# A four-layer attention chain with a state-space scan on one core: the scan as two chains of 64 batches, and another order of DMAs at the beginning and the end

## The chip, the cores and the metric

The kernel runs on one core of one Trainium2 chip. The metric is the device time of the whole program in microseconds; the kernel before has a median of 4145.38 us over 3 runs (4143.74 to 4145.70). A core has five engines that run side by side and wait for each other by semaphores: TensorE (PE in the profile, its weight loads PEld), VectorE (DVE), ScalarE (ACT), GpSimd (POOL) and SyncE (SP), which here issues nearly all DMAs. A DMA can also be issued by ACT.

## The reference

128 batches with sequences of 128 tokens of 256 features; all in float32. Four layers follow one another, each attending to the same context or to the state before:

```python
x = L0(x, ctx)         # causal self-attention, 16 heads; cross-attention; feed-forward; three layer norms
x = L1(ctx, x, ...)    # norm, attention to itself, gelu(fc1) of 4 channels, fc2, norm, attention again
x = L2(x, ctx)         # H_real + softmax(H_real @ H_fake.T) @ H_fake
# L3: multi-head attention on normed inputs, a residual, and then
xn = _layernorm(x, g2, beta2)
U = (xn @ W_in.T + b_in) @ Bmat                      # 64 states per token
def step(s, u_t):
    s = jax.nn.silu(s @ A.T) + u_t
    return (s, s)
_, states = jax.lax.scan(step, zeros, U.transpose(1, 0, 2))   # over the 128 tokens
ssm_out = jnp.einsum('tbs,sh->bth', states, Cmat)
mod = program_probs.mean(axis=1) @ W_prog.T + b_prog          # program_probs: 128 x 128 x 64
return x + ssm_out + mod[:, None, :]
```

The scan is sequential over tokens and independent over batches.

## The kernel before, in words

The batches are worked in 64 groups of G = 2. `drive` runs every engine through 64 + 6 iterations, each with one step of every unit (`self_in`, `self_att`, `ctx_in`, `ctx_att`, `ffn`, `pair`, `real`, `mix_in`, `mix_att`, `mix_out`) for a group that lags by a fixed number of iterations; the order inside an iteration comes from the table PROGRAM, and eight PSUM banks are lent by the table BANKS. `drive` also calls extra functions ahead of a given iteration (its last argument).

Beginning. SP loads what the first attention needs (`first_loads`), then at iteration 1 the context weights (`load_ctx_weights`, L450) and at iteration 2 everything else (`load_late_weights`, L454): nine weights, 29 small rows and columns, and 16 pieces of the columns q3_b and k3_b (L462). All of these count on the semaphore `rest_in`. At iteration 3 (`PREPARED`) each engine runs `prepare()`: ACT reorders the weights q2, k2, q3, k3 (L1018) once all of `rest_in` has come; TensorE and DVE fold norms into weights and biases and make the modulation rows. For these program_probs is summed over its 128 tokens: four pieces of 1 MB (`probs_in`), loaded from ACT's queue at iteration 2 (L1026), one pair added by DVE (L1338), the other by POOL (L1543, semaphore `half_added`), their sum by DVE (L1341) and so on. The rows of all batches are stored to memory at iteration 6 and come back group by group (`load_mod`, L497, tile `mod`).

End of the loop. For each group SP loads the modulation rows, stores the finished residual (`store`, L502, tensor `residual`) and the two batches' u of 64 states by 128 tokens (`store_u`, L518, tensor `u_turned`). At iteration 68 `scan_early` (L504) waits until the buffers that the scan takes over are free and loads u (L443, tile `shared`, in the code `fresh`) and the first two residual chunks (L445, tile `turned`, in the code `res_t`) of the first 122 batches; after the last group the other 6 batches follow, and chunks 2 and 3 (L527). A chunk is 8 tokens of all 128 batches, 1 MB.

Scan. A second block. The state has 64 rows, below it 64 rows of u_t, so that one matmul of 128 rows with A.T twice over gives (silu + u) A.T: recurrence matmul L1612, Silu L1632 into the next column block of `gu` (tiles Z and X), and the output matmul L1604 with C, which DVE adds into the residual chunk (L1641). POOL copies u for four tokens at a time into `gu` (L1625). SP stores finished chunks and loads those to come (L1583, L1579). A float32 matmul is two passes, shown as two records.

Of the kernel before, what the change touches and what calls it, by code (L numbers as in the profile page):

```python
# [24 lines left out]
G = 2  # L25
# [220 lines left out]
PREP_BANKS = (0, 1, 2, 3, 4, 5)  # L246
# [16 lines left out]
def build(nc, dram):  # L263
# [6 lines left out]
    with ExitStack() as ctx:  # L270
# [99 lines left out]
        means, added, half_added, ordered = (sem(n) for n in ("means", "added", "half_added", "ordered"))  # L370
# [34 lines left out]
        def row(t):  # L405
# [7 lines left out]
        late_loads = [*((wt[n][:], weight(n)) for n in ("fc1", "fc2")), *((in_rows[n], weight(n)) for n in ("q3", "k3")),  # L413
                      *((wt[n][:], weight(n)) for n in ("v3", "o3")), (w_gate[:], weight("gate")), (w_in[:], weight("in")),
                      (b_mat[:, :, 0:NS], dram["b_mat"].rearrange("(a p) n -> p a n", p=128)),
                      *((t[:], dram["col_" + n]) for n, t in cols.items() if n not in ("q3_b", "k3_b")),
                      *((t[:], row(dram["row_" + n])) for n, t in rows.items() if n[0:3] not in ("ln1", "ln2")),
                      *((gate_col[32 * b:32 * b + 4, :], dram["gate_b"].rearrange("(c o) -> c o", o=1)) for b in range(G)),
                      *((w_cross[32 * b:32 * b + 5, :], dram["w_cross"]) for b in range(G)),
                      (w_prog[0:NP, 0, :], dram["w_prog"]), (w_prog[:, 1, :], row(dram["prog_b"])),  # L420
                      *((a_two[NS * k:NS * k + NS, 0:NS], dram["a_t"]) for k in range(2)),
                      *((c_two[NS * k:NS * k + NS, :], dram["c_mat"]) for k in range(2))]
        FIRST = 16 * len(first_loads)
        REST = 16 * (len(ctx_loads) + len(late_loads) + 8 * DH)
# [10 lines left out]
        vbank, obank = pbank[0:2], pbank[2:6]  # L435

        u_in, zeroed, u_ready, v_ready, g_ready, o_ready, out_ready = (
            sem(n) for n in ("u_in", "zeroed", "u_ready", "v_ready", "g_ready", "o_ready", "out_ready"))
# [1273 lines left out]
```

## Time and profile before

| what | value |
|---|---|
| median of 3 runs | 4145.38 us (4143.74 to 4145.70) |
| the profiled execution | 4143.41 us, of which the span of the trace is 4141.6 us |
| PE busy | 3924.8 us, 95% |
| ACT busy | 3527.3 us, 85% |
| DVE busy | 3346.5 us, 81% |
| POOL busy | 2858.1 us, 69% |
| DMA | 159.99 MB, 39 GB/s in the mean |
| granted TensorE clock, mean | 0.98 |

The busy figures are sums over engines that overlap; a busy TensorE is not one at its peak, since the ends of its matmuls are modelled. The span begins with the first instruction on the core and ends with the last; the device time is 1.8 us longer. The loop over the groups takes most of it, and a share over the whole span says little on the beginning, the last groups and the scan, so these were read from stretches of the trace.

### The profile page before, as it was taken

What the parts mean: (1) busy time and instruction counts of PE and PEld (TensorE: products, weight loads), DVE (VectorE), ACT (ScalarE), POOL (GpSimd) and SP (SyncE); (2) the same over time, 40 slices, a digit from 0 to 9 for tenths busy, and PEclk for the clock granted to TensorE, in tenths of its full rate; (3) what the DMA queues carried; (4) which work ended last, traced back from release to release, by engine and by line L of the source; (5) the groups of instructions that cost most, each with busy time, mean ns of one, the idle gap of its engine ahead of it and who ended that gap; (6) DMA issues with size and microseconds to landing.
All of it is one profiled execution on the core that took longest, in us unless ns stands there. A gap on an engine that the chain in (4) does not pass through costs nothing.

```text
span 4141.6 us, 110586 instructions
## 1 busy us (share of the span) xinstructions
PE 3924.8 (95%) x36667; PEld 3225.8 (78%) x36667; DVE 3346.5 (81%) x9518; ACT 3527.3 (85%) x8333; POOL 2858.1 (69%) x3173
## 2 busy tenths in 40 slices
PE   5899999999999999999999999999999999999759
PEld 4678888888888888888888888888888888887635
DVE  4688888888888888888888888888888888888534
ACT  3799999899999999999999999999999998999522
POOL 2567777777777777777777777777777777776634
PEclk7999999999999999999999999999999999999869
DMA  3010011011101101110101011001100110110037
GB/s 114 19 32 25 28 31 33 20 33 31 34 20 31 33 26 28 31 34 20 34 31 33 20 31 33 27 27 31 34 25 29 31 33 20 34 31 26 15 104 274
DMA packets 121843, 159.99 MB, mean 39 GB/s; under 512 B 12282, under 2 KB 108356, under 8 KB 116612
## 3 DMA queue, kind: packets, MB, share of 16 engines
q1 hardware_dynamic: 120708, 148.74, 11.9%
q8 instruction: 303, 4.96, 0.5%
q10 hardware_dynamic: 576, 4.19, 0.2%
q14 instruction: 256, 2.10, 0.2%
HBM read 115.01 MB, written 37.88 MB: 37 GB/s over the span
## 4 chain that ended last, share of the span: by engine, by line
PE 71%; ACT 17%; issue 6%; DVE 1%; POOL 1%; DMA 0%; ACTq 0%; SPq 0%; DVEq 0%; another core or an unknown queue 0%; POOLq 0%
PE bank L544 18%; PE bank L600 11%; PE bank L552 8%; PE bank L536 7%; PE bank L571 5%; PE bank L717 4%; ACT probT L920 3%; PE bank L763 3%; PE bank L704 3%; PE bank L634 3%; PE bank L647 3%; ACT L901 2%; PE bank L629 2%; ACT prob L901 2%; ACT HC L970 1%
## 5 line engine op out<-in xcount | busy, mean ns | idle before, releaser
L600 PE MATMUL bank<-ident,prob 128*128 128x128 f32 x5120 | 728.6, 277 | 67.3 <-ACT CR L987 26.8
L920 ACT ACTIVATE probT<-bank 128x512 f32<-128x512 f32 x1280 | 730.5, 593 | 70.1 <-PE bank L600 68.7
L600 PEld LDWEIGHTS bank<-ident,prob 128*128 128x128 f32 x5120 | 590.9, 142 | 148.8 <-issue 62.6
L891 ACT ACTIVATE turned<-bank 128x512 f32<-128x512 f32 x896 | 538.9, 602 | 186.8 <-PE bank L536 177.5
L1120 DVE TENSOR_REDUCE mx<-bank 128x4 f32<-128x512 f32 x768 | 507.6, 682 | 187.0 <-PE bank L571 184.6
L909 ACT ACTIVATE prob<-prob,mx 128x128 f32<-128x128 f32 x2048 | 650.6, 396 | 3.9 <-DVE mx L1109 3.8
L544 PE MATMUL bank<-turned,shared 128*128 128x256 f32 x2560 | 617.0, 384 | 1.2 <-ACT turned L891 1.1
L1426 POOL TENSOR_TENSOR rs_ln<-ve_ln,half 128x2 f32<-128x2 f32 x320 | 227.3, 710 | 444.5 <-DVE ve_ln L1091 444.5
L1131 DVE TENSOR_TENSOR prob<-bank,mx 128x512 f32<-128x512 f32 x768 | 520.5, 685 | 15.3 <-PE bank L600 1.9
L544 PEld LDWEIGHTS bank<-turned,shared 128*128 128x128 f32 x2560 | 470.2, 192 | 69.2 <-issue 12.1
L901 ACT ACTIVATE prob<-prob 128x512 f32<-128x512 f32 x768 | 475.6, 636 | 13.6 <-DVE prob L1131 12.7
L571 PE MATMUL bank<-shared,turned 32*128 32x256 f32 x4096 | 447.6, 402 | 3.6 <-DVE prob L1102 2.2
L1505 POOL TENSOR_SCALAR shared<-turned,half_of 128x512 f32<-128x512 f32 x256 | 399.8, 1575 | 21.4 <-ACT turned L891 21.3
L1102 DVE TENSOR_TENSOR prob<-bank,causal 128x512 f32<-128x512 f32 x512 | 344.6, 683 | 54.9 <-PE bank L600 47.7
L552 PE MATMUL bank<-shared,turned 128*128 128x256 f32 x1536 | 369.9, 384 | 1.2 <-DVE turned L1238 1.2
L1109 DVE TENSOR_REDUCE mx<-prob 128x4 f32<-128x512 f32 x512 | 346.9, 678 | 16.8
L571 PEld LDWEIGHTS bank<-shared,turned 32*128 32x128 f32 x4096 | 284.1, 185 | 82.4 <-issue 47.4
L552 PEld LDWEIGHTS bank<-shared,turned 128*128 128x128 f32 x1536 | 281.5, 190 | 55.7 <-issue 22.7
L634 PE MATMUL bank<-probT,shared 128*32 128x128 f32 x8192 | 290.9, 277 | 0.9 <-ACT probT L920 0.8
L1440 POOL TENSOR_TENSOR X<-X,row_ln_g 128x512 f32<-128x512 f32 x192 | 244.8, 1275 | 62.0 <-ACT X L970 62.0
L1516 POOL TENSOR_TENSOR prob<-prob,inv 128x512 f32<-128x512 f32 x256 | 263.3, 1039 | 4.3 <-DVE inv L1147 4.3
L634 PEld LDWEIGHTS bank<-probT,shared 128*32 128x32 f32 x8192 | 204.5, 109 | 76.4 <-issue 75.3
(238 smaller groups left out, 9003.1 us busy)
## 6 DMA issues: line engine op xcount, KB each, us to landing
shared<-in_x SPq DMA_DIRECT2D x128, 256.0 KB, 3.0
CB<-in_ctx SPq DMA_DIRECT2D x64, 256.0 KB, 4.0
CC<-in_ctx SPq DMA_DIRECT2D x64, 256.0 KB, 2.7
mod<-mod_rows SPq DMA_DIRECT2D x64, 256.0 KB, 3.7
residual<-X SPq DMA_DIRECT2D x64, 256.0 KB, 3.2
out<-turned SPq DMA_DIRECT2D x16, 1024.0 KB, 4.8
turned<-residual SPq DMA_DIRECT2D x14, 1024.0 KB, 6.8
u_turned<-us SPq DMA_DIRECT2D x128, 32.0 KB, 2.2
```

The costliest lines, as they stand in the source:

```text
L544: last = nc.tensor.matmul(t[:, m * W:(m + 1) * W], w[:, a, m * 128:(m + 1) * 128], src[:, a, :], start=(a == 0), stop=(a == DH - 1))
L552: last = nc.tensor.matmul(t[:, b * D:(b + 1) * D], src[:, a, b * S:(b + 1) * S], w[:, a, :], start=(a == 0), stop=(a == DH - 1))
L571: last = nc.tensor.matmul(t[:, a * W:(a + 1) * W], QT[p][rows_, a, b * S:(b + 1) * S], KEYS[p][rows_, a, :, b * S:(b + 1) * S], start=True ...
L600: last = nc.tensor.transpose(t[:, h * 128:(h + 1) * 128], src[:, h, :], ident[:])
L634: last = nc.tensor.matmul(t[k * 32:(k + 1) * 32, r * 128:(r + 1) * 128], VP[p][:, b, 4 * r + k, :], src[:, k, :], start=True, stop=True)
L891: nc.scalar.activation(dst, banks.of(f"{unit}.{name}")[:, 0:n], ACT.Copy).then_inc(*st["act"].mark(name))
L901: nc.scalar.activation(flat(t), flat(t), ACT.Exp, scale=SCALE[p]).then_inc(*st["act"].mark(f"exp.{b}{r}"))
L909: last = nc.scalar.activation(t[:, h, :], t[:, h, :], ACT.Exp, bias=low[:, h:h + 1], scale=1.0)
L920: nc.scalar.activation(flat(t), banks.of(f"{att}.turn.{b}{r}")[:, :], ACT.Copy).then_inc(*st["act"].mark(f"probT.{b}{r}"))
L1120: nc.vector.tensor_reduce(m[:], banks.of(f"{att}.tile.{b}{r}")[:, :].rearrange("p (h t) -> p h t", h=4), AX, ALU.max)\
L1131: nc.vector.tensor_tensor(t[:], banks.of(f"{att}.tile.{b}{r}")[:, :].rearrange("p (h t) -> p h t", h=4), maxes.of(f"{att}.max.{b}{r}")[:]. ...
L1505: last = nc.gpsimd.tensor_scalar(KEYS[p][:, :, c, :], KT[p][:], half_of[:, c:c + 1], None, ALU.mult)
```

## The change

Three parts, in one diff.

Beginning: the 7 context loads and 9 late weights are issued from ACT's queue before ACT's first instruction of the loop, and the 4 loads of program_probs right after its first reordering. SP issues the 29 small loads at iteration 1 and the 16 pieces at iteration 2. The second pair of program_probs is added by DVE. The products of `prepare()` stand in three banks in place of six.

End: `scan_early` is called by `load_mod` behind the modulation rows of group 62. `scan_late` loads what is missing of groups 61 and 62 ahead of the last store. The u of groups 62 and 63 is copied from its tile straight into the scan's buffer, and the last group's rows of chunk 0 straight from the residual tile `X6`.

Scan: each step is done for two halves h of 64 batches, with PSUM banks and semaphores of their own. The output of half 1 goes to the upper 64 partitions of the same bank.

```diff
@@ -243,7 +243,7 @@
-PREP_BANKS = (0, 1, 2, 3, 4, 5)
+PREP_BANKS = (0, 1, 2)
...
@@ -447,14 +449,12 @@
-                def load_ctx_weights():
-                    for t, src in ctx_loads:
+                def load_small():
+                    sp.wait_ge(prep, 2)
+                    for t, src in small_loads:
                         sp.dma_start(t, src).then_inc(rest_in, 16)
-                def load_late_weights():
-                    sp.wait_ge(prep, 2)
-                    for t, src in late_loads:
-                        sp.dma_start(t, src).then_inc(rest_in, 16)
+                def load_biases():
...
+                    if g == NG - 2:
+                        scan_early()
                 def store(g):
+                    if g == NG - 1:
+                        scan_late()
                     for w in latest(mix_out["pool"].done("mod", g)):
                         sp.wait_ge(*w)
                     sp.dma_start(res_g[g], nat["X6"][:]).then_inc(res_out.sem, 16)
+                    if g == NG - 1:
+                        for b in range(G):
+                            sp.dma_start(res_t[0][B - G + b:B - G + b + 1, :, :], nat["X6"][0:TC, b, :]).then_inc(res_in[0], 16)
...
+                def scan_late():
+                    for w in latest(u_out.done(NG - 3), res_out.done(NG - 2)):
+                        sp.wait_ge(*w)
+                    sp.dma_start(fresh[:, EARLY:EARLY + G, :], u_t[:, EARLY:EARLY + G, :]).then_inc(u_in, 16)
+                    for k in (0, 1):
+                        sp.dma_start(res_t[k][EARLY:B - G, :, :], res_d[EARLY:B - G, k * TC:(k + 1) * TC, :]).then_inc(res_in[k], 16)
                 def store_u(g):
                     for w in latest(mix_out["dve"].done("u", g)):
                         sp.wait_ge(*w)
                     for b in range(G):
-                        sp.dma_start(u_g[g][b], us[NS * b:NS * b + NS, :]).then_inc(u_out.sem, 16)
+                        to = u_g[g][b] if g < NG - 2 else fresh[:, G * g + b, :]
+                        sp.dma_start(to, us[NS * b:NS * b + NS, :]).then_inc(u_out.sem, 16)
...
                                    pair=dict(load=load_pair), mix_out=dict(load=load_mod, store=store, store_u=store_u)), "sp",
-                      {1: load_ctx_weights, 2: load_late_weights, MOD_STORED: store_modulation, NG + LAGS - 2: scan_early})
-                for w in latest(res_out.done(NG - 1), u_out.done(NG - 1)):
+                      {1: load_small, 2: load_biases, MOD_STORED: store_modulation})
+                for w in latest(res_out.done(NG - 1)):
                     sp.wait_ge(*w)
-                scan_input(sp, slice(EARLY, B), (0, 1))
+                sp.dma_start(res_t[1][B - G:B, :, :], res_d[B - G:B, TC:2 * TC, :]).then_inc(res_in[1], 16)
                 for k in (2, 3):
                     sp.dma_start(res_t[k], res_d[:, k * TC:(k + 1) * TC, :]).then_inc(res_in[k], 16)
...
                                                         scale=L0_HD ** -0.5 if name == "q1" else 1.0)
                         last.then_inc(ordered, 1)
-                def load_probs():
-                    ctxb_v = ctxb_d.rearrange("b (c s) n -> b c s n", c=4)
-                    for c, t in enumerate(probs_in):
-                        act.dma_start(t, ctxb_v[:, c, :, :]).then_inc(probs_here, 16)
                 def prepare():
                     act.wait_ge(rest_in, REST)
                     in_order("q2", "k2", "q3", "k3")
+                for t, src in ctx_loads + late_weights:
+                    act.dma_start(t, src).then_inc(rest_in, 16)
                 act.wait_ge(first_in, FIRST)
                 in_order("q1", "k1")
+                ctxb_v = ctxb_d.rearrange("b (c s) n -> b c s n", c=4)
+                for c, t in enumerate(probs_in):
+                    act.dma_start(t, ctxb_v[:, c, :, :]).then_inc(probs_here, 16)
...
                     dve.wait_ge(probs_here, 64)
                     t = probs_in[0]
                     nc.vector.tensor_tensor(t, t, probs_in[1], ALU.add).then_inc(added, 1)
-                    dve.wait_ge(added, 1)
-                    dve.wait_ge(half_added, 1)
+                    nc.vector.tensor_tensor(probs_in[2], probs_in[2], probs_in[3], ALU.add).then_inc(added, 1)
+                    dve.wait_ge(added, 2)
                     nc.vector.tensor_tensor(t, t, probs_in[2], ALU.add).then_inc(added, 1)
                     for k in range(4):
                         n = S // 8 >> k
-                        dve.wait_ge(added, k + 2)
+                        dve.wait_ge(added, k + 3)
                         nc.vector.tensor_tensor(t[:, 0:n, :], t[:, 0:n, :], t[:, n:2 * n, :], ALU.add).then_inc(added, 1)
-                    dve.wait_ge(added, 6)
+                    dve.wait_ge(added, 7)
                     nc.vector.tensor_tensor(msum[:, 1, 0:NP], t[:, 0, :], t[:, 1, :], ALU.add).then_inc(means, 2)
...
                 def rows_here():
-                    pool.wait_ge(probs_here, 64)
-                    nc.gpsimd.tensor_tensor(probs_in[2], probs_in[2], probs_in[3], ALU.add).then_inc(half_added, 1)
                     pool.wait_ge(rest_in, REST)
...
-                def output(n):
-                    if n >= 4:
+                def output(n, h):
+                    if n >= 4 and h == 0:
                         pe.wait_ge(out_ready, n - 3)
-                    nc.tensor.matmul(obank[n % 4][:, 0:D], gu[n // 4 % 4][:, n % 4, :], c_two[:], start=True, stop=True).then_inc(o_ready, 1)
+                    nc.tensor.matmul(obank[n % 4][side[h], 0:D], gu[n // 4 % 4][:, n % 4, side[h]], c_two[:], start=True, stop=True)\
+                        .then_inc(o_ready, 1)
                 pe.wait_ge(zeroed, 1)
                 for n in range(1, S):
                     if (n - 1) % 4 == 0:
                         pe.wait_ge(u_ready, (n - 1) // 4 + 1)
-                    if n >= 2:
-                        pe.wait_ge(g_ready, n - 1)
-                    nc.tensor.matmul(vbank[n % 2][:, 0:B], a_two[:], gu[(n - 1) // 4 % 4][:, (n - 1) % 4, :], start=True, stop=True)\
-                        .then_inc(v_ready, 1)
-                    output(n - 1)
-                pe.wait_ge(g_ready, S - 1)
-                output(S - 1)
+                    for h in range(2):
+                        if n >= 2:
+                            pe.wait_ge(g_ready[h], n - 1)
+                        nc.tensor.matmul(vbank[h][n % 2][0:NS, 0:B // 2], a_two[:, 0:NS], gu[(n - 1) // 4 % 4][:, (n - 1) % 4, side[h]],
+                                         start=True, stop=True).then_inc(v_ready[h], 1)
+                        output(n - 1, h)
+                for h in range(2):
+                    pe.wait_ge(g_ready[h], S - 1)
+                    output(S - 1, h)
             @block.gpsimd
             def _(pool):
                 pool.wait_ge(u_in, 32)
+                for w in latest(u_out.done(NG - 1)):
+                    pool.wait_ge(*w)
                 for c in range(S // 4):
                     if c >= 4:
-                        pool.wait_ge(o_ready, 4 * (c - 4) + 4)
+                        pool.wait_ge(o_ready, 8 * (c - 4) + 8)
                     nc.gpsimd.tensor_scalar(gu[c % 4][NS:2 * NS, :, :], fresh[:, :, 4 * c:4 * c + 4].rearrange("p b t -> p t b"),
                                             1.0, None, ALU.mult).then_inc(u_ready, 1)
             @block.scalar
             def _(act):
                 for n in range(1, S):
-                    act.wait_ge(v_ready, n)
-                    nc.scalar.activation(gu[n // 4 % 4][0:NS, n % 4, :], vbank[n % 2][0:NS, 0:B], ACT.Silu).then_inc(g_ready, 1)
+                    for h in range(2):
+                        act.wait_ge(v_ready[h], n)
+                        nc.scalar.activation(gu[n // 4 % 4][0:NS, n % 4, side[h]], vbank[h][n % 2][0:NS, 0:B // 2], ACT.Silu).then_inc(g_ready[h], 1)
             @block.vector
                 def add(n, k, kb, t):
-                    dve.wait_ge(o_ready, n + 1)
+                    dve.wait_ge(o_ready, 2 * n + 2)
                     nc.vector.tensor_tensor(res_t[kb][:, t, :], res_t[kb][:, t, :], obank[k][:, 0:D], ALU.add).then_inc(out_ready, 1)
                 def body(c, k, r):
                     for t in range(TC):
                         n = c * TC + t
                         if t == 1:
-                            dve.wait_ge(res_in[k], 16 * (r + (2 if k < 2 else 1)))
+                            dve.wait_ge(res_in[k], 16 * (r + (4, 3, 1, 1)[k]))
                         if at_least(n, 1):
```

On TensorE, the scan's first steps. Z is the tile of states and u, a_two is A.T, c_two is C. Before:

```order
L1612 MATMUL bank<-Z,a_two 128x128 [waits u_ready,zeroed]
L1604 MATMUL bank<-c_two,Z 128x256
L1612 MATMUL bank<-Z,a_two 128x128 [waits g_ready]
L1604 MATMUL bank<-c_two,Z 128x256
L1612 MATMUL bank<-Z,a_two 128x128 [waits g_ready]
L1604 MATMUL bank<-c_two,Z 128x256
```

And of the changed kernel, where L1631 is the recurrence and L1621 the output:

```order
L1631 MATMUL bank<-Z,a_two 64x64 [waits u_ready,zeroed]
L1621 MATMUL bank<-c_two,Z 64x256
L1631 MATMUL bank<-Z,a_two 64x64
L1621 MATMUL bank<-c_two,Z 64x256
L1631 MATMUL bank<-Z,a_two 64x64 [waits g_ready0]
L1621 MATMUL bank<-c_two,Z 64x256
L1631 MATMUL bank<-Z,a_two 64x64 [waits g_ready1]
L1621 MATMUL bank<-c_two,Z 64x256
```

The recurrence of each half waits for the Silu of its own half only, and stands behind the output of the other half.

On SP's queue, the last groups of the loop before (L497 modulation rows, L502 residual out, L518 u out, L443 and L445 the scan's u and residual in, L527 chunks 2 and 3):

```order
L443 DMA shared<-u_turned 64x15616 [waits ctx_in_dve_3,self_att_pe_2,ctx_att_pe_4,self_att_pool_2,ffn_pe_4,self_in_dve_2,u_out,self_in_pool_1,res_out,self_in_dve_1,self_in_pe_1]
L445 DMA turned<-residual 122x2048 x2
L497 DMA mod<-mod_rows 128x512 [waits mix_out_pool_6]
L502 DMA residual<-X 128x2x256 [waits mix_out_pool_6]
L518 DMA u_turned<-us 64x128 [waits mix_out_dve_6]
L518 DMA u_turned<-us 64x128
L497 DMA mod<-mod_rows 128x512 [waits mix_out_pool_6]
L502 DMA residual<-X 128x2x256 [waits mix_out_pool_6]
L518 DMA u_turned<-us 64x128 [waits mix_out_dve_6]
L518 DMA u_turned<-us 64x128
L443 DMA shared<-u_turned 64x768 [waits u_out,res_out]
L445 DMA turned<-residual 6x2048 x2
```

The same place in the changed kernel (L506 residual out, L536 u out, L445, L447 and L526, L528 the scan's inputs, L510 the direct copies):

```order
L497 DMA mod<-mod_rows 128x512 [waits mix_out_pool_6]
L445 DMA shared<-u_turned 64x15616 [waits ctx_in_dve_3,self_att_pe_2,ctx_att_pe_4,self_att_pool_2,ffn_pe_4,self_in_dve_2,u_out,self_in_pool_1,res_out,self_in_dve_1,self_in_pe_1]
L447 DMA turned<-residual 122x2048 x2
L506 DMA residual<-X 128x2x256 [waits mix_out_pool_6]
L536 DMA shared<-us 64x128 [waits mix_out_dve_6]
L536 DMA shared<-us 64x128
L497 DMA mod<-mod_rows 128x512 [waits mix_out_pool_6]
L526 DMA shared<-u_turned 64x256 [waits res_out,u_out]
L528 DMA turned<-residual 4x2048 x2
L506 DMA residual<-X 128x2x256 [waits mix_out_pool_6]
L510 DMA turned<-X 1x8x256 x2
L536 DMA shared<-us 64x128 [waits mix_out_dve_6]
```

Group 62's modulation rows stand ahead of the two loads of 122 rows, those of group 63 still behind them, and u goes to `shared` instead of `u_turned`.

On ACT, the beginning of the changed kernel (before, the table load and the first reordering were its first instructions, and the loads of in_ctxb came behind four evacuations):

```order
L1046 DMA w_v<-in_w_v 128x2x256
L1046 DMA w_o<-in_w_o 128x2x256
L1046 DMA w_gate<-in_w_gate 128x2x4
L1046 DMA X<-in_w_in 128x2x256
L1046 DMA H<-in_b_mat 128x2x64
L1036 ACT_TABLE_LOAD
L1036 ACTIVATE shared<-turned 128x256 [waits first_in]
L1036 ACTIVATE shared<-turned 128x256 x3
L1051 DMA shared<-in_ctxb 128x2048 x3
L1051 DMA turned<-in_ctxb 128x2048
```

These are the last five of its 16 weight loads; ACT's first activation stands behind all of them.

## Rows read from the trace of the kernel before

**Rows 1.** The page: shares of the last chain; groups, as busy, mean ns.

```profile
PE 71%; ACT 17%; issue 6%; DVE 1%; POOL 1%; DMA 0%; ACTq 0%; SPq 0%; DVEq 0%; another core or an unknown queue 0%; POOLq 0%
...
L920 ACT ACTIVATE probT<-bank 128x512 f32<-128x512 f32 x1280 | 730.5, 593 | 70.1 <-PE bank L600 68.7
...
L634 PE MATMUL bank<-probT,shared 128*32 128x128 f32 x8192 | 290.9, 277 | 0.9 <-ACT probT L920 0.8
```

**Rows 2.** Stretches: length, then busy PE, PEld, DVE, ACT, POOL, clock, DMA, GB/s.

```profile
40.20:60.20 20.00, 0.07 (x4) 0.00 (x0) 0.00 (x0) 3.10 (x10) 0.00 (x0) 0.58 0.37 77
...
87.70:3930.00 3842.30, 3727.01 (x35603) 3092.28 (x35604) 3230.78 (x9230) 3438.52 (x8083) 2755.14 (x3102) 0.99 0.10 28
...
4030.10:4137.30 107.20, 106.18 (x494) 64.15 (x493) 52.58 (x125) 33.27 (x123) 54.59 (x29) 1.00 0.72 265
```

**Rows 3.** Timeline, beginning: start, length, instruction, [idle before it and releaser].

```profile
4.61 0.47 SPq L452 DMA_DIRECT2D turned<-in_w_q  x1
...
6.71 1.34 ACT L1018 ACTIVATE shared<-turned 128x256 f32<-128x256 f32 x4 [4.70 <-DMA NF<-in_causal]
...
18.29 0.38 SPq L476 DMA_DIRECT2D shared<-in_x  x1
...
21.66 3.76 SPq L457 DMA_DIRECT2D w_v<-in_w_v  x1
...
52.28 3.67 SPq L462 DMA_DIRECT2D col_k_b<-in_col_k_b  x8
57.15 1.34 ACT L1018 ACTIVATE shared<-turned 128x256 f32<-128x256 f32 x4 [16.89 <-DMA col_k_b<-in_col_k_b]
...
60.24 1.11 PE L647 MATMUL bank<-ident,outT 128*128 128x128 f32 x4 [19.98 <-ACT outT L935]
```

**Rows 4.** Timeline, the preparation on DVE.

```profile
65.53 2.28 DVE L1338 TENSOR_TENSOR shared<-shared 128x2048 f32<-128x2048 f32 x1
...
72.43 3.27 DVE L1341 TENSOR_TENSOR shared<-shared 128x2048 f32<-128x2048 f32 x1 [4.62 <-POOL shared L1543]
```

**Rows 5.** Timeline, the last groups of the loop.

```profile
3937.07 33.36 SPq L497 DMA_DIRECT2D mod<-mod_rows  x1
...
3989.07 0.18 DVE L1147 RECIPROCAL inv<-den 128x4 f32<-128x4 f32 x1
3995.80 1.26 POOL L1539 TENSOR_TENSOR X<-X,mod 128x512 f32<-128x512 f32 x1 [24.40 <-issue]
...
3998.23 4.03 POOL L1516 TENSOR_TENSOR prob<-prob,inv 128x512 f32<-128x512 f32 x4
...
4012.23 1.26 POOL L1539 TENSOR_TENSOR X<-X,mod 128x512 f32<-128x512 f32 x1 [1.35 <-ACT H L970]
```

**Rows 6.** DMA from 3957 to 3994: queue's packets, MB, share; issue, KB, landing.

```profile
q1 hardware_dynamic: 366, 2.18, 14.4%
...
mod<-mod_rows SPq DMA_DIRECT2D x1, 256.0 KB, 58.6
```

**Rows 7.** The chain that ended last, before the scan: start, length, what.

```profile
4016.24 1.90 DMA u_turned<-us
...
4018.21 4.17 DMA shared<-u_turned
```

**Rows 8.** Timeline, one step of the scan.

```profile
4080.48 0.27 ACT L1632 ACTIVATE X<-bank 64x128 f32<-64x128 f32 x1 [0.58 <-PE bank L1612]
4080.80 0.30 PEld L1612 LDWEIGHTS bank<-X,a_two 128*128 128x128 f32 x2 [0.33 <-ACT X L1632]
...
4081.33 0.27 ACT L1632 ACTIVATE Z<-bank 64x128 f32<-64x128 f32 x1 [0.58 <-PE bank L1612]
```

**Rows 9.** Lines L1612 and L1604: duration ns min/median/max, first and last start, shape.

```profile
L1612 PE MATMUL bank<-Z,a_two x128: 275/348/552, 4024.5 to 4129.4; 128*128 128x128 f32 x128
...
L1604 PE MATMUL bank<-c_two,Z x128: 379/382/634, 4025.1 to 4129.8; 128*128 128x256 f32 x128
```

**Rows 10.** DMA from 4060 to 4120: queue's packets, MB, share of 16 engines.

```profile
q1 hardware_dynamic: 2497, 18.23, 83.5%
```

More of the change, by code:

```diff
@@ L369, in build @@
         first_in, rest_in, probs_here, prep, mods, turned_b = (sem(n) for n in ("first_in", "rest_in", "probs_here", "prep", "mods", "turned_b"))
-        means, added, half_added, ordered = (sem(n) for n in ("means", "added", "half_added", "ordered"))
+        means, added, ordered = (sem(n) for n in ("means", "added", "ordered"))
         steps = {u: {e: Steps(sem, u, e) for e in ENGINES} for u in UNITS}
@@ L412, in build @@
                      *((rows[n][:], row(dram["row_" + n])) for n in ("ln1_g", "ln1_b", "ln2_g", "ln2_b"))]
[L413 to L422, printed above, removed]
+        late_weights = [*((wt[n][:], weight(n)) for n in ("fc1", "fc2")), *((in_rows[n], weight(n)) for n in ("q3", "k3")),
+                        *((wt[n][:], weight(n)) for n in ("v3", "o3")), (w_gate[:], weight("gate")), (w_in[:], weight("in")),
+                        (b_mat[:, :, 0:NS], dram["b_mat"].rearrange("(a p) n -> p a n", p=128))]
@@ new lines, in build @@
+        small_loads = [*((t[:], dram["col_" + n]) for n, t in cols.items() if n not in ("q3_b", "k3_b")),
+                       *((t[:], row(dram["row_" + n])) for n, t in rows.items() if n[0:3] not in ("ln1", "ln2")),
+                       *((gate_col[32 * b:32 * b + 4, :], dram["gate_b"].rearrange("(c o) -> c o", o=1)) for b in range(G)),
+                       *((w_cross[32 * b:32 * b + 5, :], dram["w_cross"]) for b in range(G)),
+                       (w_prog[0:NP, 0, :], dram["w_prog"]), (w_prog[:, 1, :], row(dram["prog_b"])),
+                       *((a_two[NS * k:NS * k + NS, 0:NS], dram["a_t"]) for k in range(2)),
+                       *((c_two[NS * k:NS * k + NS, :], dram["c_mat"]) for k in range(2))]
@@ L434, in build @@
                  for n in range(NB)]
-        vbank, obank = pbank[0:2], pbank[2:6]
-        u_in, zeroed, u_ready, v_ready, g_ready, o_ready, out_ready = (
-            sem(n) for n in ("u_in", "zeroed", "u_ready", "v_ready", "g_ready", "o_ready", "out_ready"))
+        vbank, obank = (pbank[0:2], pbank[6:8]), pbank[2:6]
+        u_in, zeroed, u_ready, o_ready, out_ready = (sem(n) for n in ("u_in", "zeroed", "u_ready", "o_ready", "out_ready"))
+        v_ready, g_ready = ([sem(f"{n}{h}") for h in range(2)] for n in ("v_ready", "g_ready"))
+        side = [slice(B // 2 * h, B // 2 * h + B // 2) for h in range(2)]
         res_in = [sem(f"res_in{n}") for n in range(NB)]
@@ L790, in prepare @@
                 def prepare():
-                    b_cols, b_v3, b_u, b_ub, b_turn, b_o = (pbank[n] for n in PREP_BANKS)
+                    b_fold, b_mod, b_o = (pbank[n] for n in PREP_BANKS)
                     for w in latest(*(banks.free(n) for n in PREP_BANKS)):
@@ L823, in prepare @@
                     for a in range(DH):
-                        last = nc.tensor.transpose(b_turn[:, a * 128:(a + 1) * 128], rows["v3_b"][:, a * 128:(a + 1) * 128], ident[:])
+                        last = nc.tensor.transpose(b_fold[:, a * 128:(a + 1) * 128], rows["v3_b"][:, a * 128:(a + 1) * 128], ident[:])
                     last.then_inc(turned_b, 1)
                     pe.wait_ge(means, 4)
-                    nc.tensor.matmul(b_u[:, 0:D], msT[0:NP, 0, 0:128], w_prog[0:NP, 0, :], start=True, stop=True).then_inc(means, 1)
+                    nc.tensor.matmul(b_mod[:, 0:D], msT[0:NP, 0, 0:128], w_prog[0:NP, 0, :], start=True, stop=True).then_inc(means, 1)
                     pe.wait_ge(turned_b, 2)
@@ L1332, in prepare @@
                 def prepare():
-                    b_cols, b_v3, b_u, b_ub, b_turn, b_o = (pbank[n] for n in PREP_BANKS)
+                    b_fold, b_mod, b_o = (pbank[n] for n in PREP_BANKS)
                     dve.wait_ge(rest_in, REST)
```

34 lines of the change are left out of this document (17 added, 17 removed).

## The prediction

> **What bounds the kernel now.** I read the page first: TensorE holds 71% of the chain that ended last [rows 1]. Most of that is the loop over 64 groups, which the change leaves as it is: 3842.3 us between 87.7 and 3930 [rows 2]. What can move is the 299.3 us around it, so I took a table of stretches next and looked for low TensorE shares: 0.07 us of work from 40.20 to 60.20, and the scan, 107.2 us with TensorE counted busy all through [rows 2]. The timeline, narrowed to beginning, end of the loop and scan, gave the rest.
>
> In the beginning TensorE stands 19.98 us behind an evacuation of ScalarE (ACT); ACT waits 16.89 us for the last bias column, col_k_b [rows 3]. SP issues these loads one by one until 55.95 us, some 0.47 us each, and 3.76 for one that found the queue full [rows 3]. It is bound by issue, not by bytes.
>
> At the end of the loop SP's load of group 62's modulation rows takes 33.36 us to issue and 58.6 to land [rows 5, 6]. It is queued behind two residual loads of 122 rows, during which the queue's packets fill 14.4% of the 16 engines [rows 6]: about two of them. POOL waits 24.40 us for it [rows 5].
>
> The scan step is a ring: Silu 0.27, 0.05 to the weight load, and from there 0.53 to the next Silu (4080.80 to 4081.33) [rows 8]. That is 0.85. Over the whole stretch it is 0.86: 494 passes, four a step, fill 106.18 us [rows 2]; the rest is the wait for a new block of u every fourth step.
>
> **Beginning.** Sixteen weight loads go from SP to ACT's queue and are issued from 0.7 us on. SP issues its 29 small loads where it had the context weights (4.61 us [rows 3]): 29 by 0.47 is 13.6, so the next group's x leaves at about 18.3, as it did (18.29). The 16 bias columns take 16 by 0.46 (3.67 for eight [rows 3]), from 19.2 to 26.6. With landing and a fuller queue all is there at about 31 instead of 57. ACT came to its wait at 57.15 - 16.89 = 40.26. Without the wait TensorE resumes at 40.26 + (60.24 - 57.15) = 43.4 [rows 3]. But ACT has 16 DMAs to issue before its first activation, 16 by 0.47 = 7.5 us: that moves from 6.71 to 9 at the earliest, and to 15 if two issues stall as SP's did. The four probability loads (1.9 us) now stand ahead of its first evacuation. I take +5 (3 to 8): TensorE resumes at 48.4, -11.9. In the preparation DVE waits 4.62 us for POOL's half of a sum [rows 4]; it does that add itself now, in 2.28 like its own of that size: -2.3. Both stand on the chain to the loop. Beginning: -14 (8 to 19). That the preparation uses three banks in place of six costs nothing: it has the same products in the same order, each in a part of a bank of its own.
>
> **End of the loop.** The modulation load of group 62 goes ahead of the residual loads and lands at once. Then DVE is late next: its last reciprocal ends at 3989.07 + 0.18 = 3989.25. Three of POOL's four scalings (4.03 / 4 = 1.01 each) are done by then, the last ends at 3990.3 instead of 3998.23 + 4.03 = 4002.26: -12 [rows 5]. Group 63's rows now queue behind the slow loads, which end by 3937.07 + 58.6 = 3995.7; they are needed at 4012.23 - 12 = 4000.2, so 4.5 us of cover remain [rows 5, 6]. The last u went to memory (1.90) and came back (4.17) [rows 7]; one DMA now puts it into the scan's buffer, at 1.9 to 2.5: -4, and +0.5, since SP issues three DMAs more ahead of it. End: -15.5 (12 to 17).
>
> [...]
>
> **Scan.** A step has four matmuls instead of two: for each half the recurrence, 64x64, and the output with 64 weight columns; and two Silus of 64 columns. A pass of 256 columns has 382 ns, the shortest of 128 has 275 [rows 9]: 0.84 ns a column and 168 ns from the last column to the end. Passes of 64 columns stream in 0.053. The ring of one half is Silu 0.216 (0.27 for 128 columns and 0.593 for 512 [rows 1, 8], so 0.84 ns a column), 0.05, and 0.53 less three times 0.053, 0.37: 0.64. Every matmul is two passes. The array's first 64 columns hold both recurrences and the output of half 0: 4 by 0.053 and 2 by 0.214, 0.64, with an uncovered weight load 0.67. The output of half 1 uses the other 64 columns and can run beside them, if tiles overlap. They do: 8192 passes of 128 columns on tiles of 32 cost 290.9 us [rows 1], 0.036 each where one alone streams 0.106. What no row shows is when a waiting engine is told, if a later instruction on another tile ends first.
>
> DMA has a floor of its own: 83.5% of 60 us in the scan [rows 10], 69.8 steps: 0.72 us a step if the engines never rest, 0.80 with a tenth of idleness. The ends are 0.67 and 0.92 (rival A). I take 0.77, between the two DMA figures: (0.86 - 0.77) by 127 = -11.4. What runs beside it still fits: an add of DVE and half a us of POOL's copies a step. Behind the last step the stores are less far along than now: +1. Scan: -10.4 (-23 to +9).
>
> **Sum** against the profiled execution of 4143.41 (span 4141.6): 4143.4 - 14 - 15.5 - 10.4 = 4103.5. The median of the runs shown, 4145.4, is 2 us above that execution, which makes 4105.
>
> **Rivals.**
> A. Passes end in program order, across tiles too. The next recurrence of half 0 can't end before the output of half 1 ahead of it: 0.107, 0.427, and the second output with half of it uncovered, 0.85 with a weight load and up to 0.92 a step. The scan is 8 slower, not 11 faster: 4105 + 19 = 4124. With no overlap at all it is 4 by 0.053 and 4 by 0.214, 1.09 with loads: +29, 4146. For A: in before no tile's product is waited for while another tile works. Against it: the 0.036 us. 0.15 for the two.
> [...]
> B. DMA decides the scan. Stores and loads hold each other up and a chunk comes late: 0.80 to 0.86 a step, 4109 to 4117. For it: 83.5% already [rows 10]; against it: the engines hold at 0.72. 0.2.
> C. The beginning's gain is given back. ACT's 20 issues stall in a full queue as SP's did for 3.76 us, and the first groups run late by as much as the biases are early: -5 instead of -14, 4114. Against it: ACT's wait has 16.89 us to give. 0.12.
> D. Slower: going from one half of the array's columns to the other empties it, 168 ns at each of two changes a step, with nothing beside: 1.07 + 0.34 = 1.41, (1.41 - 0.86) by 127 = +70 and the 1 behind the last step, against 29.5 gained: 4187. It decides from 1.08 us a step on. Against it the 0.036 us. 0.04.
> The forecast holds 0.49.
>
> **Numbers.** 4105 us. The range reaches to B, C and most of A at one end and a step of 0.68 with the beginning at its best at the other: 4090 to 4126. 0.2%, 8.3 us, is about what a measurement of this kernel tells from no change: faster 0.93; within it 0.03, A without any overlap; slower 0.04, D.
>
> **What would show it.** ACT's ordering of the weights, now at 57.15, at 43 to 49 with no long wait before it; no wait of DVE for POOL in the preparation; no issue of a modulation load over 1 us; POOL's copy of the first u at about 3993 instead of 4018.21 + 4.17 = 4022.4; Silus of one half 0.77 apart. At 0.92 the start of a recurrence would be held to the end of the output before it; under B the waits would be DVE's for a residual chunk. Wrong would be: the step above 0.86, group 63's modulation rows late, or ACT idle for more than 10 us in the first 20.

## The result, and the profile after

The changed kernel takes 4110.4 us (median of 4 runs, 4108.1 to 4112.6) against 4144.6 for the kernel before in the same runs: 0.9919 times as long, 95% interval 0.9906 to 0.9933. The forecast was 4105 us, with a range of 4090 to 4126. The profiled execution took 4108.45 us with a span of 4106.6, which is 35.0 less than the span before, where 39.9 were forecast. The table puts the difference where the traces show it. It compares starts: DVE's write of the first u of the loop (tile `us`), that of group 62, the scan's first matmul, the end.

| part | forecast | measured in the traces |
|---|---|---|
| beginning, to the first u (294.06, now 284.31) | -14 | -9.8 |
| loop, from there to the u of group 62 (3979.50, now 3973.21) | 0 | +3.5 |
| last group and direct loads (scan starts at 4024.53, now 4005.57) | -15.5 | -12.7 |
| scan (117.1, now 101.0) | -10.4 | -16.0 |

The 3.5 us in the loop aren't the change's. From the first u to that of group 62 the trace of before has 3685.4 us and that of the changed kernel 3688.9; over all traces below, whose loops are the same, it lies between 3684.9 and 3691.9, and three kernels with one part of the change each have 3688.5 to 3688.9.

The start of the loop varies as much, and the -9.8 is one pair of traces. The six traces with the changed beginning have their first u at 283.2 to 288.8, the four with the beginning of before at 291.6 to 294.1, and the means are 6.5 us apart. That agrees with the 5.9 us that the beginning alone gains by its medians (begin_alone, below): about 6 us of the 9.8 are the change's.

The beginning, on the timeline of the changed kernel (start, length, instruction, what it waited for):

```profile
5.86 1.83 SPq L455 DMA_DIRECT2D col_n_w<-in_col_n_w  x1
...
11.86 0.23 DVE L1404 TENSOR_SCALAR causal<-NF 128x128 f32<-128x128 f32 x1 [7.90 <-DMA NF<-in_causal]
...
13.60 1.28 ACT L1036 ACT_TABLE_LOAD   x1 [13.60 <-issue]
14.89 0.42 ACT L1036 ACTIVATE shared<-turned 128x256 f32<-128x256 f32 x1
...
28.68 0.51 SPq L476 DMA_DIRECT2D shared<-in_x  x1
...
35.48 4.82 SPq L462 DMA_DIRECT2D col_k_b<-in_col_k_b  x8
...
49.87 1.33 ACT L1036 ACTIVATE shared<-turned 128x256 f32<-128x256 f32 x4
...
52.95 0.66 PE L665 MATMUL bank<-ident,outT 128*128 128x128 f32 x4 [2.66 <-ACT outT L953]
```

Against [rows 3]: the wait of 16.89 us for col_k_b is gone and TensorE waits 2.66 us where it waited 19.98. But ACT's first activation moved from 6.71 to 14.89. ACT's 16 issues last from 0.73 to 13.57, 12.8 us where 7.5 were reckoned, and its table load of 1.28 us, which ran at 0.73 before, now stands behind them, at 13.60. The first loads landed late too (the causal mask is used at 11.86, and before at 6.71), and the next group's x is issued at 28.68 and not 18.29. TensorE resumes at 52.95, where 48.4 was forecast and 60.24 stood before.

The preparation on DVE, and the last group, on the same timeline:

```profile
57.78 2.28 DVE L1356 TENSOR_TENSOR shared<-shared 128x2048 f32<-128x2048 f32 x1
...
59.98 2.28 DVE L1357 TENSOR_TENSOR shared<-shared,turned 128x2048 f32<-128x2048 f32 x1
...
62.30 3.24 DVE L1359 TENSOR_TENSOR shared<-shared 128x2048 f32<-128x2048 f32 x1
...
3964.67 1.26 POOL L1557 TENSOR_TENSOR X<-X,mod 128x512 f32<-128x512 f32 x1
...
3982.33 2.04 POOL L1534 TENSOR_TENSOR prob<-prob,inv 128x512 f32<-128x512 f32 x2 [0.48 <-DVE inv L1165]
...
3988.42 3.75 PE L570 MATMUL bank<-w_o,turned 128*128 128x256 f32 x8 [0.93 <-ACT turned L944]
...
4000.46 1.17 SPq L536 DMA_DIRECT2D shared<-us  x2
```

DVE goes from its own add to the sum in 4.52 us, where [rows 4] had 6.90. POOL adds the modulation rows of group 62 without a wait (24.40 us in [rows 5]), and its last two scalings now end right behind DVE's last reciprocal. The output projection, though, takes 3.75 us. The timeline of before, and its stretch from there to the scan:

```profile
3999.42 3.81 PE L600 MATMUL bank<-ident,prob 128*128 128x128 f32 x16 [18.43 <-POOL prob L1516]
...
4005.49 1.97 PE L552 MATMUL bank<-w_o,turned 128*128 128x256 f32 x8 [0.91 <-ACT turned L926]
```

```profile
3999.40:4024.50 25.10, 9.29 (x68) 6.47 (x68) 2.45 (x9) 5.96 (x9) 6.98 (x8) 0.64 0.27 66
```

There the same eight passes take 1.97 us. The stretches of the changed kernel (columns as in [rows 2]) say why:

```profile
3980.00:4005.50 25.50, 12.11 (x68) 8.20 (x68) 5.47 (x17) 6.61 (x11) 7.16 (x7) 0.50 0.21 70
4005.50:4011.00 5.50, 5.43 (x38) 4.22 (x40) 1.56 (x4) 1.84 (x9) 5.34 (x3) 0.58 0.58 243
4011.00:4102.50 91.50, 90.77 (x985) 70.34 (x984) 52.35 (x125) 52.87 (x245) 55.26 (x29) 1.00 0.84 311
```

TensorE's granted clock is 0.50 in the whole last stretch of the loop, where it had a mean of 0.64 before. What differs ahead of it: behind its wait of 18.43 us TensorE had 16 passes of transposes on end, 3.81 us without a pause, since POOL's scalings were late together; now these come four or eight at a time with pauses between. That this raised the clock is my reading of the two timelines, no more.

The scan's steady pace is read from SP's stores, one for each chunk of 8 steps; eight chunks lie between these two:

```profile
4031.98 0.34 SPq L1599 DMA_DIRECT2D out<-turned  x1
...
4078.92 0.34 SPq L1599 DMA_DIRECT2D out<-turned  x1
```

64 steps in 46.94 us are 0.733 us a step, against 0.86 before and 0.77 in the forecast. From 4011 to 4100 no engine waits for a DMA in this trace; the waits are for one another's results.

### The profile page after: what moved, and what is told of

It is laid out like the page before. It is cut to its first block and busy times, and to the rows that moved or that the text cites. A ratio compares the mean times of both kernels' runs of the same rounds, so it can differ in the third digit from the quotient of the medians.

```text
span 4106.6 us, 111739 instructions
## 1 busy us (share of the span) xinstructions
PE 3913.2 (95%) x37177; PEld 3233.6 (79%) x37177; DVE 3349.2 (82%) x9519; ACT 3547.9 (86%) x8460; POOL 2854.5 (70%) x3172
## 5 line engine op out<-in xcount | busy, mean ns | idle before, releaser
L618 PE MATMUL bank<-ident,prob 128*128 128x128 f32 x5120 | 728.8, 277 | 56.9 <-ACT CR L1005 26.9
L919 ACT ACTIVATE prob<-prob 128x512 f32<-128x512 f32 x768 | 475.5, 636 | 13.0 <-DVE prob L1149 12.1
L1127 DVE TENSOR_REDUCE mx<-prob 128x4 f32<-128x512 f32 x512 | 347.3, 679 | 16.8
```

The costliest lines, as they stand in the source:

```text
L618: last = nc.tensor.transpose(t[:, h * 128:(h + 1) * 128], src[:, h, :], ident[:])
L919: nc.scalar.activation(flat(t), flat(t), ACT.Exp, scale=SCALE[p]).then_inc(*st["act"].mark(f"exp.{b}{r}"))
```

## The experiments

All times are medians beside runs of the kernel before on the same chip, and the ratio is to those.

| run | us | before | ratio, 95% interval |
|---|---|---|---|
| begin_alone | 4139.3 | 4145.1 | 0.9984 (0.9975 to 0.9994) |
| end_alone | 4133.1 | 4145.1 | 0.9969 (0.9956 to 0.9982) |
| scan_alone | 4128.3 | 4145.1 | 0.9956 (0.9939 to 0.9973) |
| spread | 4113.1 | 4145.1 | 0.9916 (0.9899 to 0.9932) |
| small_first | 4108.8 | 4144.5 | 0.9916 (0.9900 to 0.9933) |
| warm | 4108.2 | 4144.5 | 0.9912 (0.9895 to 0.9929) |
| half_chunks | 4107.0 (one run) | 4144.5 | |
| one_tile | 4156.1 (one run) | 4144.5 | |
| early112 | 4137.4 | 4144.8 | 0.9980 (0.9971 to 0.9990) |
| balanced | 4106.3 | 4144.8 | 0.9906 (0.9890 to 0.9923) |
| rroo | 4103.2 | 4144.8 | 0.9898 (0.9881 to 0.9914) |
| best | 4097.0 | 4143.2 | 0.9885 (0.9868 to 0.9901) |

**The parts one by one.** Each is the kernel before with one of the change's three parts.

> Before with the beginning alone changed. If the parts don't touch one another it gains what the two traces differ by at the loop's start, 9.7 us: 4135 us. If the 3 us that the later groups of the pair of traces lost belong to the beginning (another phase of the loop) it is 4138.

> Before with the end of the loop alone changed. The difference of the traces there is 12.7 us: 4132 us, with the last output projection of the loop at the half clock (3.7 us for 8 passes and not 2.0). If the clock was lost only because of the changed beginning, it is 15.5: 4129.

> Before with the scan alone in two halves: 16 us less, 4129 us, and 0.734 us a step. If the faster step in the changed kernel needed its earlier loads it stays above 0.76 and 4133.

They gain 5.9, 12.1 and 16.8 us by the medians, 34.8 together; the whole gains 34.1. So they add. Forecast were 14, 15.5 and 10.4. In end_alone the output projection takes 3.75 us as well, so the clock is lost with the changed end alone. scan_alone has the same 0.733 a step.

**Why the end stood still before.** The kernel before with one number changed:

```diff
-        EARLY = B - 3 * G
+        EARLY = B - 8 * G
```

> Before, with the early loads of u and residual for the first 112 batches in place of 122 and the other 16 at the end; the modulation rows of group 62 stay behind them. If 33 us of issue are the 122 rows on two of 16 engines, 112 rows spread over 16, the modulation load issues in under 6 us, POOL's wait goes and the last scalings end at 3990 as in the changed kernel: 12 us less, minus up to 1 for the longer last loads: 4133. If the queue is slow for another reason, nothing changes: 4145.

On SP's timeline of early112 the load that took 33.36 us to issue takes half a microsecond:

```profile
3936.24 1.04 SPq L445 DMA_DIRECT2D turned<-residual  x2
3937.33 0.53 SPq L497 DMA_DIRECT2D mod<-mod_rows  x1
```

From the u of group 62 to that of 63 it has 26.8 us, the changed kernel 26.9 and before 35.9. That much, 9 us, the two loads of 122 rows cost, and either the order or the number of rows cures it. The forecast of 4133 was missed by 4: the longer last loads took 2.7 us and not 1 (11.9 from the last u to the scan and not 9.2), and the clock is lost here too (output projection 3.75 us).

**The clock.** The changed kernel with matmuls that nothing reads:

```diff
+                def warm(t, k):
+                    for _ in range(k):
+                        nc.tensor.matmul(t[:, 0:128], ident[:], ident[:], start=True, stop=True)
...
+                            warm(t, 9)
...
+                            warm(t, 10)
...
+                        warm(pbank[7], 16)
```

> The changed kernel with 9, 10 and 16 more matmuls of the identity on TensorE in the last group (ahead of its first transposed probability, ahead of h6T, and behind u), into banks that are free then; nothing reads them. If the 2.8 us that the end of the loop fell short are the granted clock, the last output projection takes 2.0 and not 3.75 us and the scan's first five steps run at 0.73: 4 to 5 us less, 4106. If the clock stays low, it is the same time or up to 1 us more.

The 9 ahead of the first transposes didn't help: on TensorE's timeline of warm the output projection stays at 3.75, so how the clock came back in before stays open. The 10 ahead of h6T (the last transposes of the loop) and the 16 behind u did:

```profile
3993.76 3.75 PE L574 MATMUL bank<-w_o,turned 128*128 128x256 f32 x8 [0.92 <-ACT turned L958]
...
4002.26 0.63 PE L558 MATMUL bank<-ident,H 128*128 128x128 f32 x4 [2.00 <-ACT H L1002]
4003.73 0.66 PE L810 MATMUL bank<-turned,w_u 128*64 128x128 f32 x8 [0.84 <-ACT turned L923]
```

These took 1.08 and 1.12 in the changed kernel. The stretch of the scan's first steps in warm (columns as above) has the full clock:

```profile
4010.60:4016.00 5.40, 5.33 (x59) 4.10 (x60) 2.53 (x6) 2.77 (x14) 5.24 (x3) 1.00 0.62 258
```

59 passes where 5.50 us at 0.58 held 38. In the trace the scan is 2.0 us shorter (99.0 against 101.0). The median falls by 2.3, but the intervals of the two ratios overlap (0.9895 to 0.9929, and 0.9906 to 0.9933), so the gain is shown by the trace and not by the times. The share that the output projection lost, 1.8 us, wasn't won back.

**What sets the scan's step.** Two runs that leave something out, and one that only reorders.

```diff
-                    sp.dma_start(out_d[:, bass.ds(c * TC, TC), :], res_t[k]).then_inc(chunk_out[k], 16)
+                    sp.dma_start(out_d[0:64, bass.ds(c * TC, TC), :], res_t[k][0:64]).then_inc(chunk_out[k], 16)
```

(and the loads alike)

> The changed kernel with stores and loads of residual chunks inside the scan for the first 64 batches only: half of the scan's bytes, and half of the output isn't written. If DMA (94.9% busy at 0.734 us a step) sets the step it falls to the ring or the array, 0.64 to 0.67, 8 us less in all; if the order on TensorE sets it, it stays at 0.73.

The stores of half_chunks, and the DMA queue of half_chunks (4040 to 4090) and of the changed kernel (4040 to 4095), as packets, MB, share of 16 engines:

```profile
4035.95 0.49 SPq L1599 DMA_DIRECT2D out<-turned  x1
...
4082.96 0.49 SPq L1599 DMA_DIRECT2D out<-turned  x1
```

```profile
q1 hardware_dynamic: 1352, 8.85, 77.5%
```

```profile
q1 hardware_dynamic: 2657, 19.29, 94.9%
```

0.735 a step: DMA doesn't set it. And the share is no measure of room: with 8.9 MB in 50 us and not 19.3 in 55 the engines are still counted busy for 77.5%.

```diff
-                    nc.tensor.matmul(obank[n % 4][side[h], 0:D], gu[n // 4 % 4][:, n % 4, side[h]], c_two[:], start=True, stop=True)\
+                    nc.tensor.matmul(obank[n % 4][0:64, h * D:h * D + D], gu[n // 4 % 4][:, n % 4, side[h]], c_two[:], start=True, stop=True)\
```

> The changed kernel with the output of half 1 computed on the array's first 64 columns too, into the bank's second 256 columns; DVE goes on adding the first 256, so half of the output is wrong. If the two outputs overlap in the changed kernel because they are on different columns, the step here is 4 by 0.053 + 4 by 0.214 = 1.07 us or more, 43 us more in all. If they don't overlap, the step stays 0.73.

Its stores:

```profile
4045.07 0.34 SPq L1599 DMA_DIRECT2D out<-turned  x1
...
4115.25 0.34 SPq L1599 DMA_DIRECT2D out<-turned  x1
```

70.18 us for 64 steps, 1.097 each. The outputs on the two halves of the array overlap, and that is worth 0.36 us a step. Rival A's second form had 1.09 for this.

```diff
                                          start=True, stop=True).then_inc(v_ready[h], 1)
+                    for h in range(2):
                         output(n - 1, h)
```

> The changed kernel with both recurrences of a step issued ahead of both outputs. If the step of 0.734 is 0.67 of streaming plus a release that has to come in program order behind the other tile's output, both outputs now end together and the step falls to 0.67 to 0.70: 4 to 8 us less, 4104. If a recurrence is held by the wait of the other half ahead of it, it rises to 0.8: 8 us more. If neither, 0.73.

Its stores, and its DMA queue from 4040 to 4090:

```profile
4035.71 0.34 SPq L1599 DMA_DIRECT2D out<-turned  x1
...
4078.80 0.34 SPq L1599 DMA_DIRECT2D out<-turned  x1
```

```profile
q1 hardware_dynamic: 2642, 19.27, 99.5%
```

0.673 a step, 7.2 us less in the median, and none of its runs (4102.1 to 4106.1) reaches those of the changed kernel. So the changed kernel's order cost 0.06 a step. The DMA engines are counted busy for 99.5% here; between 4030 and 4090 still no engine waits for a DMA. Where it lies, one step of the changed kernel on TensorE shows (starts; x2 or x3 gather passes, also of both halves):

```profile
4062.54 0.33 PE L1631 MATMUL bank<-X,a_two 128*64 128x64 f32 x2
...
4062.71 0.66 PE L1621 MATMUL bank<-c_two,X 128*64 128x256 f32 x3
...
4063.14 0.28 PE L1631 MATMUL bank<-X,a_two 128*64 128x64 f32 x2
...
4063.30 0.30 PE L1631 MATMUL bank<-X,a_two 128*64 128x64 f32 x2
```

A recurrence at 4062.54, the output 0.17 behind it, the other recurrence 0.43 behind that, the next step's 0.16 behind that, 0.76 in this step. The output's 0.43 agrees with the prediction's 0.427 of streaming; the recurrences take 0.17 and 0.16 and not 0.107. On the timeline of PEld the weight load of the output between them begins at 4062.65, 0.11 behind the recurrence, and the output 0.06 behind its load; that this late load costs the rest is my estimate, and no run shows it. That the interleaving itself costs this, and not a release in program order, I read from these starts. The expectation had named the release, and its number came; no run separates the two. What program order does not do is on the timeline of rroo, in which both outputs stand behind both recurrences:

```profile
4060.59 0.43 PE L1621 MATMUL bank<-c_two,Z 128*64 128x256 f32 x1
4060.65 0.22 PE L1631 MATMUL bank<-Z,a_two 128*64 128x64 f32 x1
```

A pass of an output starts ahead of the last pass of a recurrence that comes before it in the program.

**The beginning.** Three ways to issue the same loads. In spread ACT issues its 16 behind its first four evacuations, and the four of program_probs behind the last of these (the diff is shortened):

```diff
-                for t, src in ctx_loads + late_weights:
-                    act.dma_start(t, src).then_inc(rest_in, 16)
+                                xT=behind(evac(...), 7), q=behind(evac(...), 2), k=behind(evac(...), 5), v=behind(evac(...), 2, True)
```

> The changed kernel, but ACT issues its 16 weight loads behind the first four evacuations (7, 5, 2, 2) and the four loads of program_probs behind those, in place of ahead of its first activation. If the 8.2 us by which that activation became late are paid in full, TensorE resumes at 44 to 46 and not 52.95: 7 to 9 us less than the changed kernel, 4102. If the loads are bound by bytes and the bias columns then come later, the wait for rest_in returns and 3 us or less are gained.

A miss. ACT starts at 6.57, but its issues take longer while they go on (0.45 us at 9.29, 1.99 at 19.24 and 2.01 at 21.25), and its evacuations stand behind them (timeline of spread):

```profile
14.78 0.60 ACT L909 ACTIVATE turned<-bank 128x512 f32<-128x512 f32 x1 [4.90 <-issue]
14.80 4.41 ACTq L1055 DMA_DIRECT2D shared<-in_w_fc  x2
...
24.72 0.60 ACT L909 ACTIVATE turned<-bank 128x512 f32<-128x512 f32 x1 [9.35 <-issue]
```

The first u of the loop comes at 288.58. That is 4.3 us later than in the changed kernel's trace, but within the 283.2 to 288.8 of all traces with its beginning; the median, 2.7 us above the changed kernel's, doesn't tell the two apart either. So nothing was gained. The other two put the weights back on SP: small_first issues context weights and small loads, x, late weights, biases; balanced holds 7 of the small loads back behind x, and leaves ACT's four big loads at iteration 2.

```diff
-                    for t, src in small_loads:
+                    for t, src in ctx_loads + small_loads[0:22]:
...
+                    for t, src in small_loads[22:] + late_weights:
+                        sp.dma_start(t, src).then_inc(rest_in, 16)
```

> The changed kernel with all weights back on SP: context weights and small loads first, then the next group's x, then the nine late weights, then the bias columns; ACT issues only the four loads of program_probs. If what the changed beginning lost is that ACT's loads took the DMA engines from the first loads (its first activation at 14.9 and not 6.7), ACT starts at 6.7 again, the bias columns are there at about 43 and TensorE resumes at 46 to 47: 6 us less than the changed kernel, 4105. If the bytes alone decide when the bias columns are there, it resumes after 50 and nothing is gained.

> The changed kernel with every load but those of program_probs on SP: context weights and 22 small loads ahead of the next group's x, then 7 small ones, the late weights and the bias columns; program_probs from ACT where they were before, at iteration 2. If the next x (28.68 us in the changed kernel, 31.26 in small_first) and ACT's first activation are both at their old places, 18.3 and 6.7, TensorE resumes at 44 to 47: 6 to 8 us less than the changed kernel, 4103. If the late weights collide with the 4 MB of program_probs and the bias columns come at 50, nothing is gained.

ACT starts at 6.6 and 6.5 as expected, but the 6 to 8 us aren't there: the first u of the loop is at 281.9 in small_first, 1.4 us before the earliest with the changed kernel's beginning, and at 285.1 in balanced, in their midst. The median of small_first is 1.6 lower, that of balanced 4.1. The interval of balanced's ratio overlaps the changed kernel's, and its one trace has a loop 2.3 us shorter, which lies within what the loop varies by, so that gain is neither sure nor explained. In both TensorE waits for the next x, here balanced:

```profile
34.95 1.08 PE L556 MATMUL bank<-ident,shared 128*128 128x128 f32 x4 [6.38 <-DMA shared<-in_x]
...
49.79 0.42 ACT L1038 ACTIVATE shared<-turned 128x256 f32<-128x256 f32 x1 [1.23 <-DMA col_k_b<-in_col_k_b]
```

That x was issued at 21.97 and was used 13 us later, with the 4 MB of program_probs issued from 17.89 on, three of the four pieces ahead of it. Each order moves the wait to another load. Whether bytes or packets limit them wasn't tried.

**All together.** rroo, balanced and warm in one kernel:

> The changed kernel with three edits together: both recurrences of a scan step ahead of both outputs, the loads as in balanced, and the additional matmuls of warm. If the three don't touch one another they give 7.2, 4.1 and 2.3 us less than the changed kernel's 4110.4: 4097. In the first steps of the scan the faster order and the higher clock gain together, so it may be 1 us less again; if at 0.67 us a step the DMA engines (99.5% busy in rroo) hold the scan, one of them is worth less: 4099.

4096.95 us (4095.8 to 4097.6), 13.5 less than the changed kernel and the fastest of all, at the 4097 expected. Its trace has 0.673 a step and, from the scan's first step on, the full clock.

## Why the prediction was right

The sum came out 5.4 us low, with the sign of each of the three parts right. That it came so near is in part luck: by the medians of the single parts the beginning gained 8.1 us less than forecast and the end 3.4 less, and the scan 6.4 more.

Beginning, -14 against -9.8 in the pair of traces and -5.9 by begin_alone's median, which is below the 8 to 19 of the forecast. The step "all is there at about 31" was off, it was 40, and it didn't matter, as ACT reached the wait at 49.87. "I take +5 (3 to 8)" was the mis-sized term: TensorE resumes 9.5 us behind the 43.4, at 52.95, and in five other traces with this beginning between 52.31 and 56.20. ACT's first activation moved by 8.2, with issues of 0.80 us in the mean where 0.47 was taken and a table load that the sum didn't have behind them; and the next x moved by 10 us, of which TensorE saw 1.7. One of the signs of being wrong was there: the profile has ACT idle until 13.60, since issues don't count as busy. Behind both stands a wrong sentence, "bound by issue, not by bytes". SP's small loads needed up to 1.83 us instead of 0.47 while ACT's weights came in, and in spread, small_first and balanced, to issue earlier or elsewhere moves the wait to another load. Rival C had slow issues of ACT's, and -5 for them, which is what begin_alone gained. That a full queue makes an issue slow, as the prediction has it of the 3.76 us, isn't shown: the traces have the length of the issues (3.29 us for two of ACT's at 4.46) and not its cause. The preparation's -2.3 is -2.4.

End, -15.5 against -12.7. The mechanism, mod's load out from behind the 122 rows, held: from the u of group 62 to the end of the last scaling it was 22.8 us and is 11.2, 11.6 less where 12 were forecast, and early112 takes the same 9 us from group 62 to 63 by another cure. The direct copies gave 3.7, where 3.5 were forecast (4 less the half us for SP's issues). What wasn't in the sum is TensorE's clock: at 0.50 the output projection takes 1.8 us more and the values ahead of it 0.7. I had taken the durations behind the wait from a stretch with another clock. Group 63's modulation rows, with 4.5 us of cover reckoned, came in time.

Why 122 rows are slow isn't shown, only that they are. From 3957 to 3963, behind the load of u, the queue moves 1.44 MB in early112 (112 rows) and its packets fill 86.3% of the 16 engines; before (122 rows) it moves 0.31 MB and fills 12.4%. The modulation load behind the residual loads takes 0.53 us to issue in early112 and not 33.36.

Scan, -10.4 against -16.0. I had 0.67 for the array and the ring, then took 0.77 "between the two DMA figures". That was the other mis-sized term: the busy share of the engines isn't work, and half_chunks keeps the pace with half of the bytes. The array's 0.67 was the right term, with 0.06 on top for the order of the products, and rroo runs at 0.673; the 0.03 in it for an uncovered weight load is an estimate that no run shows apart. That the 0.06 are late weight loads isn't shown. Rival A (0.92, and 1.09 without overlap) is out in its first form: a step of 0.733, and the next recurrence starts 0.16 behind the last, while the other half's output, 0.43 long by the profile's modelled ends, is under way. B is out by half_chunks and D by the step itself, 0.73 against 1.41.

With passes that start and end in program order the prediction's sum gives a step of 0.85 and more. The runs have 0.73 and 0.67, and rroo's timeline has an output's pass start at 4060.59, ahead of a recurrence's at 4060.65 that comes before it in the program.

## What to carry to other kernels

Durations behind a wait are taken at the clock granted there; when the wait goes, look whether TensorE will still have it (here the output projection took 1.97 us with a mean of 0.64 and 3.75 at 0.50, and 2.5 us of 12 went that way). Don't take the busy share of the DMA engines for a bound: look whether any engine waits for a DMA, and halve the bytes and see whether the time moves. Before a few us at one place are credited to a change, compare several traces: the start of this loop varies by up to 5.5 us among kernels with the same beginning. And when two chains share TensorE, issue the short products that others wait for first, both of them, and the long ones behind: the same instructions in another order were worth 7 us of 101.

## What the runs showed of the hardware

Products of 64 weight columns on the two halves of the array run beside each other: 0.733 us a step in the scan, and 1.097 where both outputs are on one half. The DMA engines' share in the scan is 94.9% for 19.3 MB in 55 us, 77.5% for 8.9 MB in 50, and 99.5% for 19.3 MB in 50. A load of 256 KB, issued at 21.97, was used 13 us later, with 4 MB on another queue (balanced). SP's small loads, 0.43 to 0.47 us each for most of them before, took up to 1.83 in the changed kernel, where ACT issued weights beside them, and ACT's 16 issues took 12.8 to 14.3 us in the six traces that have them. And with 26 matmuls without a reader, put where TensorE would have waited, its granted clock was 1.00 in the first steps of the scan, where it was 0.58 without.

In the scan of before, the 127 recurrence products of float32 stand as 254 records and the 128 output products as 256: two records, the "passes" of this text, for each. POOL copies u in 32 instructions of 64x512, four tokens of 128 batches each, 1.94 us in the mean. SP's 16 stores of 1 MB take 4.8 us from issue to landing in the median, and the 14 loads of 1 MB 6.8.
